# Results of the first experts: plain stores at the tokens' row addresses and gathers by GpSimd, instead of scatters and plain loads

## What is computed

```python
probs = softmax(x @ gate_weight.T)                  # 32 experts
top_vals, top_idx = top_k(probs, 8)
renorm = top_vals / sum(top_vals)
keep = sum(cumsum(renorm) < 0.8) + 1                # so at most 7 experts are kept
rw = top_vals * (arange(8) < keep); rw /= sum(rw)
for e in range(32):
    g, u = split(x @ gate_up_proj[e].T)             # 96 columns each
    acc += (silu(g) * u) @ down_proj[e].T * combine[:, e]
```

## Time and profile before

| | |
|---|---|
| median of 3 runs | 1060.76 us (1055.97 to 1062.89) |
| profiled execution | 1061.58 us |
| its span, first to last instruction | 1059.8 us |
| mean granted TensorE clock | 0.923 of full speed |
| PE busy | 863.0 us, 81% |
| POOL busy | 623.9 us, 59% |
| DVE busy | 579.2 us, 55% |
| ACT busy | 555.7 us, 52% |
| bytes moved by DMA | 181.64 MB |

### The profile page before, as it was taken

The page is one execution under the profiler, slowest core; times in us unless marked ns, Lnnn a source line. Parts: engine busy times, 40 slices in busy tenths (PEclk is TensorE's granted clock), DMA queues, the critical chain, the costliest instruction groups (busy, mean ns, idle before and its releaser), DMA issues. The chain is left out here.

```text
span 1059.8 us, 20650 instructions
## 1 busy us (share of the span) xinstructions
PE 863.0 (81%) x5512; PEld 648.8 (61%) x5512; DVE 579.2 (55%) x2104; ACT 555.7 (52%) x1124; POOL 623.9 (59%) x600
## 2 busy tenths in 40 slices
PE   5999989982789999996378997978756899999960
PEld 4566656641669899995243443534326798999850
DVE  4566786875563222235776478674725522223774
ACT  6333466650345555564267767675623555555530
POOL 2465548776777777775820010374764777777773
PEclk9999999995799999998679999999886999999995
DMA  9700002262779877774340110125336798767984
GB/s 342 261 1 1 1 32 85 93 241 85 247 264 304 273 236 226 216 250 132 137 140 35 35 36 36 51 107 220 126 118 199 264 307 275 233 218 238 369 258 167
DMA packets 93231, 181.64 MB, mean 171 GB/s; under 512 B 18985, under 2 KB 73788, under 8 KB 92736
## 3 DMA queue, kind: packets, MB, share of 16 engines
q1 hardware_dynamic: 68544, 114.19, 33.5%
q0 software_dynamic: 24576, 66.13, 17.1%
HBM read 96.34 MB, written 92.27 MB: 178 GB/s over the span
## 5 line engine op out<-in xcount | busy, mean ns | idle before, releaser
L1333 POOL DMA_INDIRECT result_rows<-ys,result_slots x288 | 289.7, 1006 | 96.8 <-issue 81.5
L1010 POOL DMA_INDIRECT expert_rows<-route_rows,index x224 | 221.5, 989 | 71.1 <-issue 65.2
L1991 ACT ACTIVATE b_probs<-ps 128x1024 f32<-128x1024 f32 x128 | 127.7, 1031 | 35.3 <-PE ps L1840 34.3
L1488 PE MATMUL ps<-w_gu,g_xts 128*128 x576 | 107.7, 330 | 1.5 <-issue 0.7
L1488 PE MATMUL ps<-w_gu,f_xts 128*128 x576 | 107.4, 330 | 1.1 <-issue 1.1
L1488 PEld LDWEIGHTS ps<-w_gu,g_xts 128*128 128x128 f32 x576 | 93.2, 193 | 3.0 <-issue 2.9
L1488 PEld LDWEIGHTS ps<-w_gu,f_xts 128*128 128x128 f32 x576 | 93.2, 192 | 2.3 <-issue 2.1
L1852 PE MATMUL ps<-b_probs,b_v_pad 128*32 128x512 f32 x512 | 76.3, 671 | 12.9 <-issue 6.8
L1585 DVE SCALAR_TENSOR_TENSOR f_h<-ps,f_xs,f_gate 128x96 f32<-128x96 f32 x144 | 39.1, 313 | 83.4 <-ACT f_gate L1540 82.1
L1551 ACT COPY ys<-ps 128x512 f32<-128x512 f32 x144 | 83.5, 580 | 1.8 <-PE ps L1507 1.8
L1585 DVE SCALAR_TENSOR_TENSOR g_h<-ps,g_xs,g_gate 128x96 f32<-128x96 f32 x144 | 39.2, 313 | 76.1 <-ACT g_gate L1540 72.0
(11 more groups left out here) (368 smaller groups left out, 1793.4 us busy)
## 6 DMA issues: line engine op xcount, KB each, us to landing
parts<-result_rows SPq DMA_DIRECT2D x32, 896.0 KB, 5.1
f_xs<-expert_rows SPq DMA_DIRECT2D x144, 160.0 KB
g_xs<-expert_rows SPq DMA_DIRECT2D x144, 160.0 KB
expert_rows<-pad_rows SPq DMA_DIRECT2D x64, 160.0 KB
w_gu<-in_Wgu SPq DMA_DIRECT2D x1, 6144.0 KB, 19.5
expert_rows<-pad_rows SPq DMA_DIRECT2D x1, 5120.0 KB, 30.8
result_rows<-ys,result_slots POOLq DMA_INDIRECT x288, 3.3
f_w_d<-in_Wdown SPq DMA_DIRECT2D x1, 4096.0 KB, 14.8
```

The source lines that it names most:

```text
L1010: self.nc.gpsimd.indirect_dma_start(xs, bass.IndirectOffsetOnAxis(self.index[:, f, t, r:r + 1].bitcast(U32), 0), self.x_rows(f)[:, t, :], ...
L1333: self.nc.gpsimd.indirect_dma_start(self.y_dram, bass.IndirectOffsetOnAxis(self.slots[:, i, j:j + 1].bitcast(U32), 0), self.ys[:, i, j, :] ...
L1488: ins = nc.tensor.matmul(ps[:, bank_gu[u % 2], j * GU:(j + 1) * GU], xts[:, u % 2, o:o + P], w_gu[:, k, bass.ds(experts[j] * GU, GU)], sta ...
L1991: nc.scalar.activation(probs[:, u % RING, :, :], ps[:, 2 * (u % 2):2 * (u % 2) + 2, :], ACT.Exp, scale=float(HD) ** -0.5).then_inc(exp_don ...
```

## The change

1. In the first experts the results aren't scattered. SP stores each pair by two plain DMAs of 128 KB into a new table `expert_results`, at the row addresses that it read for loading the pair; it keeps these addresses in registers for 11 turns of its loop (`BEHIND`), so the store of pair `u - 11` stands behind the load of pair `u`.
2. The sum of a token tile is fed by 7 indirect DMAs by POOL (`Gathered.gather`), which read for each token the row given by `index`, rank by rank: 42 of them in the experts (tiles 0 to 5, from `u = 50` on), 70 in the attention (tiles 6 to 15). The 144 indirect scatters of results (122 in the experts, 22 in the attention) and the 16 loads of 896 KB go.
3. Six tiles are summed in the experts, at `u` = 55, 58, 61, 64, 68 and 71, ten in the attention. DVE's slot copies go in the first experts.
4. Pads of the first experts are stored by ACT, two behind each `keep_x` for `u` from 5 to 20, instead of by SP.
5. All indirect DMAs take their bounds check from a register set once in each block, instead of a number. The second experts are as before otherwise.

```diff
+class Gathered:
+    def store(self, sp, u, rows):
+        i = self.at(u)
+        for j, row in enumerate(rows):
+            sp.dma_start(self.y_rows[bass.ds(row, P), :], self.ys[:, i, j, :].bitcast(I32)).then_inc(self.stored[i], 16)
+
+    def gather(self, pool, t, r):
+        i = t % self.RING
+        if r == 0 and t >= self.RING:
+            pool.wait_ge(self.added, t - self.RING + 1)
+        self.nc.gpsimd.indirect_dma_start(
+            self.parts[:, i, r, :].bitcast(I32), None, self.y_rows,
+            bass.IndirectOffsetOnAxis(self.index[:, t // TT, t % TT, r:r + 1].bitcast(U32), 0),
+            bounds_check=self.most, oob_is_err=True).then_inc(self.loaded[i], 16)
...
             for u in range(PAIRS + 6 * TT):
                 if u < PAIRS:
                     load(u)
+                if gathered and 0 <= u - BEHIND < PAIRS:
+                    sp.wait_ge(y_ready, u - BEHIND + 1)
+                    results.store(sp, u - BEHIND, kept.pop(u - BEHIND))
                 nth = (u - PADS_AT) // PADS_EVERY
-                if (u - PADS_AT) % PADS_EVERY == 0 and 0 <= nth < E // PADS:
+                if not gathered and (u - PADS_AT) % PADS_EVERY == 0 and 0 <= nth < E // PADS:
                     store_pads(PADS * nth, PADS)
                 for t in loads_at(u):
                     load_results(t)
+            if gathered:
+                results.wait_stored(sp, PAIRS)
...
+            def store_two_pads(first):
+                if first == 0:
+                    act.wait_ge(routing.padded, 1)
+                rows = nc.values_load_multi_w_load_instructions(
+                    routing.pads[0:1, first:first + 2], engines=[mybir.EngineType.Activation], min_val=0,
+                    max_val=DUMMY - P, skip_runtime_bounds_check_because="an expert has at most every token")[1]
+                for row in rows:
+                    nc.scalar.dma_start(xs_dram[bass.ds(row, P), :],
+                                        routing.tables.pad_rows[:, :]).then_inc(pads_stored, 16)
...
                 if u < PAIRS:
                     keep_x(u)
+                if gathered and 0 <= u - TWO_PADS_AT < E // 2:
+                    store_two_pads(2 * (u - TWO_PADS_AT))
...
-                results.wait_free(dve, u)
-                i = results.at(u)
-                for j in range(2):
-                    nc.vector.tensor_copy(results.slots[:, i, j:j + 1], xs[:, u % RING, j, bass.ds(experts[j] + D + E, 1)])
+                if not gathered:
+                    results.wait_free(dve, u)
+                    i = results.at(u)
+                    for j in range(2):
+                        nc.vector.tensor_copy(results.slots[:, i, j:j + 1],
+                                              xs[:, u % RING, j, bass.ds(experts[j] + D + E, 1)])
...
                 for v in results_at(u):
                     pool.wait_ge(y_ready, v + 1)
                     results.scatter(pool, v)
-            if out_rows is None:
-                results.wait_scattered(pool, PAIRS - LATER)
+                for t in gathers_at(u):
+                    if t == 0 or LOADED[t] > LOADED[t - 1]:
+                        results.wait_stored(pool, LOADED[t])
+                    for r in range(RANKS):
+                        results.gather(pool, t, r)
...
-        def results_at(slot, b):
-            if b < 0:
-                for i in slots_of(((0, 7, 1), (17, 19, 2)), slot):
-                    yield LATE_PAIRS[i]
+        def gathers_at(slot, b):
+            first = {-1: IN_EXPERTS, 0: 2 * TT, 1: 3 * TT}
+            spans = {-1: ((0, 7, 1), (17, 24, 1)), 0: ((1, 29, 1),), 1: ((1, 29, 1),)}
+            if b in spans:
+                for k in slots_of(spans[b], slot):
+                    yield first[b] + k // RANKS, k % RANKS
...
-            sums = {-1: {9: 4, 16: 5, 26: 6, 30: 7}, 0: {1: 8, 3: 9, 13: 10, 28: 11}, 1: {13: 12, 23: 13, 27: 14, 31: 15}}
+            sums = {-1: {12: 6, 30: 7}, 0: {10: 8, 17: 9, 24: 10, 31: 11}, 1: {10: 12, 17: 13, 24: 14, 31: 15}}
...
-            for t in range(TT, NT):
-                if t == 3 * TT:
-                    results.wait_scattered(sp, TILES // 2)
-                results.load(sp, t)
...
-                    if u == 0 and first(b):
-                        results.wait_scattered(act, TILES // 2)
...
+            routing.most = nc.gpsimd.to_reg(STORED - 1)
...
+        GATHERS_AT = 50
+        SUMS_AT = (55, 58, 61, 64, 68, 71)
+        def gathers_at(u, last):
+            for t in range(0 if last else IN_EXPERTS):
+                if u == GATHERS_AT + 3 * t:
+                    yield t
```

More of the change, by code:

```diff
@@ L50 @@
 RESULTS = 19
-LATER = 11
+IN_EXPERTS = 6
 RESULTS_AT = PARTS_AT - RESULTS * 2 * D * 4
@@ L979, in __init__ @@
         self.lst_n = 0
+        self.most = STORED - 1
     CONSTANTS = 5
@@ L1313, in __init__ @@
         self.folded, self.added = sem("folded"), sem("added")
+        self.most = NT * P * RANKS - 1
     def at(self, u):
@@ L1334, in scatter @@
                 self.y_dram, bass.IndirectOffsetOnAxis(self.slots[:, i, j:j + 1].bitcast(U32), 0), self.ys[:, i, j, :],
-                None, bounds_check=NT * P * RANKS - 1, oob_is_err=False).then_inc(self.scattered[i], 16)
+                None, bounds_check=self.most, oob_is_err=False).then_inc(self.scattered[i], 16)
     def load(self, sp, t):
@@ L1428, in load @@
                     sp.wait_ge(h_ready, u - RING + 1)
-                for j, row in enumerate(rows_of(sp, u)):
+                rows = rows_of(sp, u)
+                if gathered:
+                    kept[u] = rows
+                for j, row in enumerate(rows):
                     sp.dma_start(xs[:, u % RING, j, :], xs_dram[bass.ds(row, P), :]).then_inc(loaded[u % RING], 16)
@@ L1451, in store @@
                 sp.dma_start(out_rows[:, t, :], results.X[:, t, :]).then_inc(out_stored, 16)
+            kept = {}
             wait_weights(sp)
@@ L1599, in _ @@
         def _(pool):
+            routing.most = nc.gpsimd.to_reg(STORED - 1)
+            results.most = nc.gpsimd.to_reg(STORED - 1 if gathered else NT * P * RANKS - 1)
             for u in range(PAIRS + FLUSH):
@@ L1690, in attention @@
         ROUTE_LAST = {10: 0, 11: 1, 12: 2, 13: 4, 14: 5, 15: 6, 16: 3, 17: 7, 18: 8, 19: 9, 20: 10, 21: 11, 22: 12, 23: 13, 24: 14}
-        LATE_PAIRS = range(TILES // 2 - LATER, TILES // 2)
         block = ctx.enter_context(nc.Block())
@@ L2022, in body @@
                         routing.gpsimd(pool, step, f)
-                    for v in results_at(u, b):
-                        results.scatter(pool, v)
+                    for t, r in gathers_at(u, b):
+                        results.gather(pool, t, r)
                     for f, k in scatters_at(u, b):
                         routing.scatter(pool, f, k, xs_dram)
+            routing.most = nc.gpsimd.to_reg(STORED - 1)
             norm.exponent(pool)
@@ L2035, in _ @@
             pool.wait_ge(root_set, 1)
+            results.most = nc.gpsimd.to_reg(STORED - 1)
             for slot in range(UNITS):
                 prepare(slot, 0)
-                for v in results_at(slot, -1):
-                    results.scatter(pool, v)
+                for t, r in gathers_at(slot, -1):
+                    results.gather(pool, t, r)
             batches(body)
@@ L2298, in results_at @@
         def results_at(u, scattered, last):
+            if not last:
+                return
             left = max((Routing.ALL - scattered) // 2, placed)
-            pairs = TILES // 2 if last else TILES // 2 - LATER
+            pairs = TILES // 2
             early = early_pairs(scattered)
@@ L2308, in results_at @@
                     yield v
+        def gathers_at(u, last):
+            for t in range(0 if last else IN_EXPERTS):
+                if u == GATHERS_AT + 3 * t:
+                    yield t
         def sums_at(u, last):
-            first, every, count = (59, 3, NT) if last else (66, 2, TT)
+            if not last:
+                for t, at in enumerate(SUMS_AT):
+                    if u == at:
+                        yield t
+                return
+            first, every, count = 59, 3, NT
             at = u - first
@@ L2319, in loads_at @@
         def loads_at(u, last):
-            return sums_at(u - 3, last)
+            return sums_at(u - 3, last) if last else ()
         def weights_ready(use):
@@ L2337, in program @@
                                   index)
-                results = Results(nc, lambda n: signal(f"{use}_result_{n}"), X, ys, slots, parts, y_dram)
+                if use == "f":
+                    results = Gathered(nc, lambda n: signal(f"{use}_result_{n}"), X, ys, parts, y_rows, index)
+                else:
+                    results = Results(nc, lambda n: signal(f"{use}_result_{n}"), X, ys, slots, parts, y_dram)
                 if use == "f":
```

38 lines of the change are left out of this document (34 added, 4 removed).

## The result

The changed kernel takes 1075.82 us, median of 4 runs (1073.14 to 1076.98), against 1058.53 for the kernel before: a ratio of 1.0147, 95% interval 1.0119 to 1.0175. It is slower by 1.5%; 1058.6 was forecast. (The kernel before has four runs here, one more than in the table ahead of the prediction.) The profiled execution of the changed kernel took 1073.14 us with a span of 1071.2, so in the two profiles 11.4 us lie between the spans. The medians lie 17.3 us apart: the kernel before was profiled in one of its slower executions, the changed one in its fastest. What follows places the difference of the profiles; the rest has no place in them.

A forecast was written before the change was run, and what follows sets the result against it. PE and POOL's scatters were read as two nearly equal chains, POOL ending the first experts' block. Terms summed to -2.2 us against the profiled 1061.58; against the median of 1060.76 that gave 1058.6, range 1047 to 1076.

The forecast's parts named there:

- SP's queue and its traffic: First experts: two more stores fit SP's turn, 2.7 us against a pair's 2.83; with traffic +1.5 us (0 to +18).
- The first rival: First experts: SP becomes the bound, deciding from 3.14 us a turn; up to +18 us, 1077; chance 0.17.
- Gathers: First experts: DVE may wait 0 to 3 us once for gathered tiles, and PE behind it; +1 us (0 to +5).
- The gate: Pair 26, first of the last phase: its load can go before 346 us instead of 354.06; -1.4 us (-2 to 0).
- Pads on ACT: First experts, pairs 5 to 20: ACT's pad issues and list read delay silu; +1.5 us (0 to +6).
- slot copies: First experts, pairs 5 to 14, where DVE sets the pitch: dropping the copies gains; -2 us, 2.7 at most.
- The block's end: End of the first experts: SP's wait for the last stores replaces POOL's drain; -1.3 us (-2 to +1).
- The prologue: Attention's prologue: the root's wait for POOL goes, but tile 6's sum makes DVE late instead; 0 us (-3.5 to +3).
- The third rival: Attention gains what POOL gave up, in prologue and batch 0, plus the copies, pads free: -14 us, 1047; chance 0.16.
- Batches 0 and 1: Attention: two sums move from batch 0's start to slots 10 and 17, where DVE has gaps; -1.5 us (-4 to +3).
- The bounds check: Indirect DMAs: a register saves a 29 ns MOVE each, but POOL's queue is ahead; 0, at most 5 us gain.
- second rival: Gathers at 1.5 us or more each delay the experts' tiles and the prologue: +8 us, 1067; chance 0.12.

The follow-up runs named there:

- run 5: Changed kernel with the stores of pairs 0 to 43 issued by POOL instead of SP: 1064.78 us, 1.0033 of the kernel before; run again 1063.20 us.
- Run 2: Changed kernel with the six sums of the experts three pairs later: 1074.64 us, 1.0132 of the kernel before.
- run 7: run 6 with seven tiles gathered and summed in the experts, sums from pair 52 on: 1063.24 us, 1.0025 of the kernel before.
- Run 1: Kernel before with only the pad stores of the first experts moved to ACT: 1060.32 us, 0.9992 of the kernel before.
- run 4: Changed kernel with the prologue's tile 6 sum at slot 22 and batch 1's sums at their old slots: 1068.97 us, 1.0076 of the kernel before.
- run 6: Changed kernel with the edits of run 4 and run 5 together: 1057.94 us, 0.9979 of the kernel before.
- run 9: run 7 with its seven sums later, at 54, 58, 61, 64, 68, 71 and 74: 1057.56 us, 0.9979 of the kernel before.
- run 3: Changed kernel with the stores of pairs 0 to 15 issued by POOL instead of SP: 1075.10 us, 1.0133 of the kernel before.

## Why the prediction was wrong

**SP's queue and its traffic, +1.5: it was the whole loss that can be placed, and the step that failed was the turn.** The prediction read "Two more stores make 0.54 + 4 x 0.53 + some 0.05 of gaps = 2.7 us, against a pair's 2.83. It fits, with 0.1 us to spare". 2.7 us is the turn in its quiet form, in which no issue and no list read takes longer than it does alone; it was measured again at 405.16. The mean from pair 26 to 71 was 3.06. Against a pair of 2.83 that is the sign of the whole case, and run 5 shows it: with the stores of 44 pairs taken from SP, 11 and 13 us came back. The rows shown before had the higher price, 0.76 to 0.86 us a DMA, as a bound.

The other half is what the lead can pay. "SP has a lead of 8 pairs, 22 us, and I expect it to lose 3 or 4 of them there" was about right: 19.9 us at pair 12, 10.5 at pair 26, so 9.4 lost, a little more than 3 pairs. That what was left would last was taken for granted. PE waits as soon as the lead is 7.5 to 7.7 us, so not 10.5 but 3 us could be spent. The kernel before has no more at the gate, 8.4 us, and makes 20 of it in the rows shown before, 21 loads in 18.04 us. I used them as an upper price of a DMA and not for what they are: the time in which SP earns its lead, and in which the change gives it two stores a turn.

The first rival had the right mechanism and the right side, and its upper bound of 18 held the loss. Its point of decision, 3.14 us a turn, was passed: from pair 12 to 71 the turn was 3.21. But its working, 61 x (3.21 - 2.83) - 19, gives 4 us for this turn and not 11.7, since it let the lead sink to the 3.5 of a landing. With 19.9 - 7.6 = 12.3 to spend the same sum gives 11; that this comes so near is in part luck, as the pairs from 12 to 22 took 3.06 and not 2.83.

**Gathers, +1: no term of its own.** DVE waited 7.8 us, more than the bound of 5, because the 44th pair was stored at 437 us and not at the time of pair 50. Run 2 shows that in the changed kernel this wait is the same loss once more. With SP free, gathers start at 424.74, DVE waits 0.6 us for a tile, and PE's pairs keep their pace (run 5). The pitch of the gathers was 1.32 us, not 1.29: seven of them are 9.3 us with the slower ones among them, and that matters in run 7.

**The gate, -1.4:** right in sign and about in size; 7.7 us became 5.6, which is -2.1, and in the second profiles 7.9 became 6.3, which is -1.6; the bound was -2. The loads of pair 26 went from 351.98 on and not before 346, though: not the pads held them but SP itself, which came no earlier.

**Pads on ACT, +1.5, and slot copies, -2:** together -0.5 forecast, +2 measured in pairs 0 to 24 (80.0 against 78.0 and 77.5). Run 1 has the pads with the copies left in and took 78.5. So the pads cost 0.5 to 1 alone, and a gain from the copies didn't show in any profile. That stretch took from 78.0 to 81.9 us in the profiles with stores and with pads on ACT, a spread as large as the difference, and I leave open how the 2 us divide.

**The block's end, -1.3:** about half or nothing. In line L1435 of the changed kernel ACT's drain begins at 505.7 and SP's at 509.5, 3.8 us later, where POOL let go 4.5 us after ACT's drain:

```profile
L1435 ACTq DRAIN  x2: 614/614/614, 505.7 to 1037.4; - x2
...
L1435 SPq DRAIN  x2: 7/7/7, 509.5 to 1069.1; - x2
```

That is -0.7, and the stretch from the last silu to the drain was no shorter.

**The prologue, 0:** right as a sum (+0.8 and +1.5 in the two pairs of profiles) and right in its working. DVE's and POOL's timelines of the changed kernel:

```profile
515.53 2.11 POOL L1397 DMA_INDIRECT parts<-expert_results,index  x1 [0.61 <-issue]
```

```profile
527.54 2.14 DVE L1408 TENSOR_TENSOR parts<-parts 128x768 f32<-128x768 f32 x3 [4.09 <-DMA parts<-expert_results,index]
...
537.00 1.23 DVE L2183 TENSOR_TENSOR b_raw<-b_raw,b_rrms 128x1024 f32<-128x1024 f32 x1 [0.23 <-POOL b_rrms L2098]
```

The wait of 3.49 us for POOL is down to 0.23, and 4.09 us for tile 6 stand in its place. The third rival was right that the room was there; run 4 collected 5.4 us of it by moving one sum.

**Batches 0 and 1, -1.5:** -4.1 and +2.8 in the first profiles, about -1 together. In batch 1 the sum of tile 13, at slot 17, meets a DVE without a gap. In DVE's timeline of the changed kernel:

```profile
649.06 2.40 DVE L2190 TENSOR_TENSOR b_work<-b_raw,b_work 128x1024 f32<-128x1024 f32 x2
651.38 1.42 DVE L2197 TENSOR_TENSOR b_k_stack<-b_raw,b_k_stack 128x256 f32<-128x256 f32 x4
...
654.32 2.17 DVE L1408 TENSOR_TENSOR parts<-parts 128x768 f32<-128x768 f32 x3
```

No row from 640 to 661 us has idle time before it. That this is what batch 1 loses is likely but not shown: with its sums at the old places it took 64.1 us in runs 4 and 6, but 65.9 and 66.1 in runs 7 and 9.

**The bounds check, 0:** right. The MOVE is gone, and the 52 x scatters still take 1.28 us each:

```profile
L1012 POOL DMA_INDIRECT expert_rows<-route_rows,index x52: 969/973/1171, 266.8 to 332.3; - x52
```

**The gathers run late (second rival):** their pitch in the attention stayed at 1.33 us, with single ones up to 2.11. What stretches these single ones no run shows; it moved nothing that can be measured.

The Trainium skill, DMA: Bandwidth & Descriptors, section "Issuing engines are not separate DMA queues", says that another issuer saves only the sequencer's time, usually small. The first half agrees with the runs: 88 stores moved from SP to POOL left the bytes as they were. The second doesn't hold here: the stores moved were worth 11 and 13 us, because the sequencer's time was what ran out. In the prediction the rule was set beside the pads alone, and the question that it raises for SP's queue wasn't asked.

## What to carry to other kernels

Before an issue queue gets more work, read its lead along the whole stage, as the time from a load's issue to its use, and not at one place, and read what of it can be spent before the consumer waits: here 3 us of 10.5. Where the lead is small, at a gate or behind a crowded stretch, what counts is the turn in which it must be regained, priced by its mean over many turns and not by its quiet form. Time saved ahead of a gate that opens at its own time is lost at it. If a wait that is taken away gives nothing back, look for the queue that was catching up in it. And work that only waits for a result can go to the engine that is idle at that time: here POOL stood idle for 107 us beside the queue that was too full.

## What the runs showed that I had not expected

A plain DMA costs POOL 0.54 us, against 0.97 busy and 1.28 from start to start for an indirect one. A read of two list entries into registers takes 0.46 us at best, but from 300 to 337 us, with the DMA engines busy all the time (a share of 1.00), its median was 1.3 to 1.6 us on every engine of the changed kernel that reads (ACT's, of its pads, was 1.64):

```profile
L1469 DVEq TENSOR_LOAD <-tab x11: 577/1629/2421, 302.3 to 336.5; - x11
L1469 SPq TENSOR_LOAD <-tab x10: 713/1278/1956, 299.8 to 335.1; - x10
L1469 PEldq TENSOR_LOAD <-tab x10: 541/1258/1946, 301.1 to 334.4; - x10
```

In the kernel before the medians there were 0.80, 0.93 and 0.62 us, at a DMA share of 0.88. In runs 1, 3 and 5, at shares of 0.94 and 0.95, they were between 0.94 and 1.34. In the second profile of the changed kernel, at 0.99, they were 1.46, 0.86 and 1.51, so SP's was shorter there than in run 1. That the traffic is the cause is likely but not shown.
